# A two-layer transformer kernel: q and k roles in one copy, splits in three slots, masks and row additions moved on GpSimd, and a reordered opening

## The chip, the core and the metric

The kernel runs on one core of a Trainium2 chip. The metric is device time of one execution in microseconds (us). The time before is 1002.51 us, the median of 3 runs (996.39 to 1004.47). The engines are named as the profile names them: PE (matrix multiplies) and PEld (its weight loads), DVE (VectorE), ACT (ScalarE), POOL (GpSimd), and SP, whose queue SPq issues every DMA of this kernel.

## What is computed

Two transformer layers over 4 sequences of 512 tokens with 256 channels, 16 heads of 16 channels, and a feed-forward width of 1024. Layer 0 has a modulated norm, a dense additive bias of 4 x 16 x 512 x 512 numbers and a key mask; layer 1 is causal and is blended with its input by a gate per sequence.

```python
# layer 0
emb = silu(sin_emb(timestep)) @ W_ada + b_ada; scale, shift = split(emb)
x = ln(src) * (1 + scale) + shift
scores = q @ k.T / sqrt(16) + attention_bias;  scores = where(mask, -inf, scores)
x = x + softmax(scores) @ v @ Wo + bo
x = x + gelu2(ln(x) * g2 + beta2 ...) @ W2 + b2      # gelu2(a) = a * sigmoid(1.702 a)
# layer 1, for input x
h = ln(x) * gamma1 + beta1
x1 = x + softmax(where(causal, q @ k.T / 4, -inf)) @ v @ Wo + bo
x2 = x1 + gelu(ln(x1) * gamma2 + beta2 ...) @ W2 + b2
out = x + g * (x2 - x)
```

## The kernel before

Each engine has an instruction stream written out by hand, with semaphores between them. The work runs in phases: an opening; four X phases, each the attention of one sequence in layer 0; four Y phases, each the attention of one sequence in layer 1; and an end. The order is start, X -1, X 0, Y 0, X 1, Y 1, X 2, Y 2, Y 3, end. Phase X b does the attention of sequence b + 1 in layer 0, and Y b that of sequence b in layer 1. A phase is a loop over slots: 64 in X (one query tile of one head each), 96 in Y. The dense work of other sequences (norms, projections, output, feed-forward) is woven into the slots by the table `PLANS`: a field such as `qk=46, qk_by=2` is the slot at which PE starts the first q projection and the distance to the next. On each engine a `Stream` is a generator that yields the slot at which its next piece is due. Inside an engine everything is in order, so an instruction that waits holds all behind it.

Scores need more than bf16, so q and k are each cut into three bf16 parts (high, middle, low) and multiplied with six pairs of parts in one contraction over 96 rows (`Q_ROLE`, `K_ROLE`). ACT writes the high part (`keep_high`); DVE makes the others (`split`: the remainder L1290, which also frees PE's psD bank, the middle part L1293, the low part L1295). Then SP spreads the parts over partitions by copies inside the on-chip memory (`to_roles`, L409): for each half c of the heads six copies into q6 and then six into k6. Scores of heads 0 to 7 wait for the copies of c=0, those of heads 8 to 15 for c=1. One projection has four splits (q and k of two halves).

In an X phase SP loads a 128 x 512 bias tile for each slot into a ring of 12 (L374), POOL adds the mask to it (L554, six slots ahead: `MASK_AHEAD`), DVE adds the scores and takes the row maximum (L1340), ACT subtracts (L669), PE transposes (L937), ACT takes the exponential (L678), and PE multiplies with the values (L950). In a Y phase PE makes scores (L959), DVE finds row maxima (L1355), those are cut in parts, turned by PE, copied out by ACT (L708) and put by SP into three further rows of q6 against rows of ones in k6 (`max_rows`, L414); eight heads later PE makes the transposed scores (L969), ACT the exponential (L690), POOL zeroes the upper triangle (L593), and PE multiplies with the values (L981).

At the end of a Y phase POOL runs `set_x1` (L562, x1 = input + bo) and then, where another X phase with a new sequence follows (Y 0 and Y 1), the masks of that sequence's first six tiles:

```python
the_rest(dense, Y_SLOTS)
set_x1(b)
if b + 2 < B:
    for s in range(MASK_AHEAD):
        add_mask(b + 2, s)
```

In the opening PE starts with the embedding product (L1107), DVE adds its bias (L1205), PE spreads it over partitions (L869), ACT stores it (L728), DVE modulates (L1233, L1237), PE transposes (L863) and projects q, k (L877) and v (L884). POOL meanwhile reorders the weights (L543), fills the values with ones (L624), adds masks, adds bo (L562), fills k6's rows of ones (L630) and reorders layer 1's weights (L543).

## Time and profile before

| | |
|---|---|
| median of 3 runs | 1002.51 us (996.39 to 1004.47) |
| profiled execution | 1004.48 us, its span 1002.4 us |
| PE busy | 824.2 us (82%) |
| DVE busy | 611.7 us (61%) |
| ACT busy | 497.8 us (50%) |
| POOL busy | 417.0 us (42%) |
| HBM read | 86.28 MB, 88 GB/s over the span |

The span is what the trace covers; the rest of the time lies around it. Busy shares are averages over stages with different limits. Rows below come from the chain of waits (the work that ended last, followed back), from timelines (start in us, duration in us, engine, line, operation, out<-in, count, and in brackets the idle time before and what ended it), and from groups by line.

### The profile page before, as it was taken

How to read it: one execution, taken by the hardware profiler on the slowest of the kernel's cores; microseconds unless marked ns; L12 is line 12 of the kernel's file. 1: busy time of each engine (PE TensorE's matmuls, PEld its weight loads, DVE VectorE, ACT ScalarE, POOL GpSimd, SP SyncE). 2: the span in 40 equal slices, each digit the busy share in tenths (PEclk: the TensorE clock that was granted, in tenths of full speed). 3: DMA queues.
4: the chain of work that ended last, by engine and by line, in shares of the span. 5: the costliest groups of instructions: out<-in, count | busy, mean ns of one | idle time of the engine just before them, and what ended most of it. 6: DMA issues, size and time to landing. Idle time of an engine off the chain costs nothing.

```text
span 1002.4 us, 14648 instructions
## 1 busy us (share of the span) xinstructions
PE 824.2 (82%) x4830; PEld 492.6 (49%) x4830; DVE 611.7 (61%) x1693; ACT 497.8 (50%) x879; POOL 417.0 (42%) x422
## 2 busy tenths in 40 slices
PE   3577888789866877898998887888999897699768
PEld 1254456447532433566645533566556363446235
DVE  5899875675757824657847843666846654536121
ACT  1167786656712355666732445667742335044421
POOL 3946459655302129486402228486601113022320
PEclk9879999999995897999998997999999999889879
DMA  8476777434550024356551035455421115100000
GB/s 252 123 235 193 225 266 200 137 105 135 151 168 1 1 64 137 116 170 199 182 155 43 2 98 145 124 170 189 150 73 43 43 44 147 43 1 2 22 1 21
DMA packets 84154, 114.70 MB, mean 114 GB/s; under 512 B 9800, under 2 KB 49516, under 8 KB 84080
## 3 DMA queue, kind: packets, MB, share of 16 engines
q1 hardware_dynamic: 84080, 113.77, 37.6%
q8 instruction: 39, 0.64, 0.3%
q14 instruction: 35, 0.29, 0.1%
HBM read 86.28 MB, written 2.10 MB: 88 GB/s over the span
## 4 chain that ended last, share of the span: by engine, by line
PE 60%; DVE 21%; issue 8%; ACT 8%; POOL 2%; SPq 1%; DMA 0%; DVEq 0%; ACTq 0%; POOLq 0%
PE psD L905 11%; PE psD L917 11%; PE psE L937 6%; PE psC L981 5%; PE psC L950 4%; PE psD L877 4%; DVE tiles L1340 4%; PE psS L929 4%; PE psD L893 3%; PE psS L959 3%; PE psE L969 3%; PE psD L884 2%; ACT prob L678 2%; ACT prob L690 2%; DVE junk L1355 2%
## 5 line engine op out<-in xcount | busy, mean ns | idle before, releaser
L554 POOL TENSOR_TENSOR tiles<-tiles,mask_neg 128x512 f32<-128x512 f32 x240 | 281.9, 1204 | 89.0 <-DMA tiles<-in_fside_Bx16xSxS 71.0
L1340 DVE CUSTOM_DVE_ANT_0 tiles<-psS,tiles 128x512 f32<-128x512 f32 x256 | 174.1, 688 | 136.2 <-PE psS L929 102.1
L669 ACT ACTIVATE tiles<-tiles,rmax 128x512 f32<-128x512 f32 x224 | 161.6, 722 | 75.7 <-DVE rmax L1340 74.6
L678 ACT ACTIVATE prob<-psE 128x512 f32<-128x512 f32 x256 | 150.9, 595 | 96.8 <-PE psE L937 88.5
L1355 DVE CUSTOM_DVE_ANT_0 junk<-psS,later 128x128 bf16<-128x128 f32 (+3 forms) x256 | 121.0, 489 | 121.3 <-PE psS L959 120.5
L937 PE MATMUL psE<-ident,tiles 128*128 128x128 f32 x1024 | 161.5, 281 | 8.3 <-ACT prob L678 6.8
L937 PEld LDWEIGHTS psE<-ident,tiles 128*128 128x128 f32 x1024 | 129.1, 145 | 64.2 <-ACT prob L678 27.1
L690 ACT ACTIVATE prob<-psE 128x512 f32<-128x512 f32 (+1 forms) x192 | 95.5, 526 | 118.2 <-PE psE L969 117.3
L905 PE MATMUL psD<-hT,w 128*128 128x512 f32 x256 | 132.8, 630 | 17.5 <-DVE work L1281 13.6
L593 POOL TENSOR_SCALAR_AFFINE_SELECT prob<-prob 128x256 f32<-128x256 f32 x128 | 53.3, 440 | 220.8 <-ACT prob L690 220.8
L917 PE MATMUL psD<-w,work 128*128 128x256 f32 x512 | 134.0, 387 | 5.8 <-ACT hT L721 4.8
L929 PE MATMUL psS<-k,q 96*128 96x512 bf16 x256 | 101.4, 399 | 32.4 <-DVE rmax L1340 32.1
L959 PE MATMUL psS<-k,q 96*128 96x128 bf16 (+3 forms) x256 | 78.5, 323 | 32.9 <-DVE rmax L1355 27.3
L559 POOL TENSOR_TENSOR rstd<-var_eps,neg_half 128x4 f32<-128x4 f32 x16 | 16.6, 1036 | 207.6 <-DVE var_eps L1176 207.6
L917 PEld LDWEIGHTS psD<-w,work 128*128 128x128 f32 x512 | 91.9, 193 | 20.7 <-ACT hT L721 6.0
L969 PE MATMUL psE<-q,k 99*128 99x512 bf16 (+3 forms) x256 | 65.5, 312 | 19.1 <-ACT prob L690 18.3
L905 PEld LDWEIGHTS psD<-hT,w 128*128 128x128 f32 x256 | 45.1, 199 | 56.8 <-issue 34.1
L950 PE MATMUL psC<-prob,vx 128*32 128x256 f32 x1024 | 64.7, 395 | 1.0 <-ACT prob L678 1.0
L959 PEld LDWEIGHTS psS<-k,q 96*128 96x128 bf16 x256 | 25.2, 100 | 77.8 <-DVE rmax L1355 50.8
L929 PEld LDWEIGHTS psS<-k,q 96*128 96x128 bf16 x256 | 25.5, 100 | 65.6 <-DVE rmax L1340 46.0
L981 PE MATMUL psC<-prob,vx 128*32 128x128 f32 (+3 forms) x512 | 49.5, 539 | 1.5 <-POOL prob L593 1.4
L750 ACT ACTIVATE work<-psD,cols 128x512 f32<-128x512 f32 x32 | 22.0, 687 | 54.7 <-PE psD L905 54.7
(112 smaller groups left out, 953.6 us busy)
## 6 DMA issues: line engine op xcount, KB each, us to landing
tiles<-in_fside_Bx16xSxS SPq DMA_DIRECT2D x256, 256.0 KB, 2.7
q<-work SPq DMA_DIRECT2D x96, 128.0 KB, 2.7
k<-work SPq DMA_DIRECT2D x96, 128.0 KB, 2.4
w<-in_L_cond_W SPq DMA_DIRECT2D x12, 1024.0 KB, 5.5
res<-in_x SPq DMA_DIRECT2D x4, 512.0 KB, 5.6
out<-x SPq DMA_DIRECT2D x4, 512.0 KB, 5.0
mask_u<-in_mask_Bx1xSxS_bk SPq DMA_DIRECT2D x4, 256.0 KB, 3.1
q<-mT SPq DMA_DIRECT2D x48, 4.0 KB, 1.7
```

Source lines behind the costliest of these rows:

```text
L554: pool.tensor_tensor(tile(b, s), tile(b, s), mask_neg[:, tile_of(s)[1], :], ALU.add).then_inc(masked_p, 1)
L669: act.activation(tile(b, s), tile(b, s), ACT.Identity, scale=-1.0, bias=rmax[0][:, s:s + 1]).then_inc(shifted_a, 1)
L678: act.activation(prob0[:, part_no % 2, j, :, s % 2 * P:(s % 2 + 1) * P], psE[:, e_no(0, b, s) % 2, :].rearrange("p (k q) -> p k q", k=T), ...
L690: act.activation(prob1[:, h % KEEP, lo:hi], psE[:, n % 2, 0:hi - lo], ACT.Exp).then_inc(e_done, 1)
L905: mm = pe.matmul(psD[:, n % 2, :], w1[:, c, f * P:(f + 1) * P], hT2[:, c, :], start=c == 0, stop=c == C - 1)
L917: mm = pe.matmul(psD[:, n % 2, t % 2 * D:(t % 2 + 1) * D], gT[:, f, t * P:(t + 1) * P], w2[:, f, :], start=f == 0, stop=f == FC - 1)
L929: pe.matmul(psS[:, n % 2, :], q6[0:ROWS, h, t * P:(t + 1) * P], k6[0:ROWS, h, :], start=True, stop=True).then_inc(s_filled, 1)
L937: mm = pe.transpose(psE[:, n % 2, kt * P:(kt + 1) * P], tile(b, s)[:, kt * P:(kt + 1) * P], ident[:, :])
L950: mm = pe.matmul(psC[j * QW:(j + 1) * QW, half * S // 2:(half + 1) * S // 2], vx[0][:, kt, at:at + QW], prob0[:, part_no % 2, j, kt, :], s ...
L959: pe.matmul(psS[:, n % 2, 0:(t + 1) * P], q6[0:ROWS, h, t * P:(t + 1) * P], k6[0:ROWS, h, 0:(t + 1) * P], start=True, stop=True).then_inc( ...
L1340: dve.tensor_tensor_reduce(tile(b, s), psS[:, n % 2, :], tile(b, s), 1.0, -3e38, ALU.add, ALU.max, rmax[0][:, s:s + 1]).then_inc(s_drained, 1)
L1355: dve.tensor_tensor_reduce(junk[:, n % 2, 0:w], psS[:, n % 2, 0:w], later[:, S - w:S], 1.0, -3e38, ALU.add, ALU.max, rmax[1][:, h * T + t: ...
```

## The change

Seven things change. (1) q6 and k6 become one tensor qk6 with q and k side by side for each head, and `to_roles` copies q's part and k's part of a role in one DMA: 6 instead of 12 copies for each half. `max_rows` has 4 copies (one for each head) instead of 3. (2) `split` yields after each of its three DVE instructions, so they fall in three slots. (3) In Y phases `set_x1` and the six first masks of the next X phase get slots of their own (`x1=`, `masks=`). (4) The rows of ones are brought by a DMA from a constant table instead of POOL's memset L630. (5) On POOL `add_bo(0)` and layer 1's `swap_columns` move behind the opening, to slots 8, 12 and 16 of X -1, and the masks wait for the first norm. (6) DVE measures and turns the first mask before it modulates. (7) PE begins with 26 products of constants (`WARM_UP`), and in Y phases `store` stands before the last `max_rows`.

```diff
+WARM_UP = 26
-    ("Y", 0): Plan(tail=(0, 1), turn=5, out=(9, 10), ln2=13, t2=20,
+    ("Y", 0): Plan(x1=60, masks=44, tail=(0, 1), turn=5, out=(9, 10), ln2=13, t2=20,
...
-    ("Y", 1): Plan(tail=(0, 2), turn=5, out=(9, 12), ln2=15, t2=32,
+    ("Y", 1): Plan(x1=66, masks=44, tail=(0, 2), turn=5, out=(9, 12), ln2=15, t2=32,
...
-    ("Y", 2): Plan(tail=(0, 3), turn=5, out=(9, 12), ln2=15, t2=28,
+    ("Y", 2): Plan(x1=66, tail=(0, 3), turn=5, out=(9, 12), ln2=15, t2=28,
...
-    ("Y", 3): Plan(tail=(1, 2), turn=5, out=(9, 10), late=(1, 3, (3, 4)), ln2=13, t2=19,
+    ("Y", 3): Plan(x1=80, tail=(1, 2), turn=5, out=(9, 10), late=(1, 3, (3, 4)), ln2=13, t2=19,
...
-                for x, (dst, roles) in enumerate(((q6, Q_ROLE), (k6, K_ROLE))):
-                    for r, w in enumerate(roles):
-                        sp.dma_start(dst[r:ROWS:ROLES, c * H // C:(c + 1) * H // C, :], part[:, c, x, w, :]).then_inc(roles_in[c], 16)
+                for r, (i, j) in enumerate(zip(Q_ROLE, K_ROLE)):
+                    pair = part_row[:, c, i:PARTS + j + 1:PARTS + j - i, :]
+                    sp.dma_start(qk6[r:ROWS:ROLES, c * H // C:(c + 1) * H // C, :, :], pair).then_inc(roles_in[c], 16)
...
-                for w in range(PARTS):
-                    sp.dma_start(q6[ROWS + w:ROWS + w + 1, g * G:(g + 1) * G, :], mT[w * G * T:(w + 1) * G * T, g % 2, :]).then_inc(m_rows, 16)
+                for j in range(G):
+                    sp.dma_start(qk6[ROWS:SHIFT, g * G + j, 0, :], mT[j * PARTS * T:(j + 1) * PARTS * T, g % 2, :]).then_inc(m_rows, 16)
...
+                yield 28
+                sp.dma_start(qk6[ROWS:SHIFT, :, 1, :].bitcast(F32), ones_dram.rearrange("w (h n) -> w h n", h=H)).then_inc(ones_in, 16)
...
+                if at.ffn:
+                    store(at.ffn[1])
                 max_rows(b, 3)
...
-                if at.ffn:
-                    store(at.ffn[1])
...
+            def residual(b, at):
+                yield at.x1
+                set_x1(b)
+
+            def first_masks(b, at):
+                for s in range(MASK_AHEAD if b < B else 0):
+                    yield at.masks + 2 * s
+                    add_mask(b, s)
...
+            pool.wait_ge(norm_ready, T)
             for s in range(MASK_AHEAD):
                 add_mask(0, s)
-            add_bo(0)
-            pool.wait_ge(bo_added, 1)
-            pool.memset(k6[ROWS:SHIFT, :, :], 1.0).then_inc(ones_set, 1)
-            pool.wait_ge(ones_set, 3)
-            swap_columns(1)
+            def first_bo():
+                yield 8
+                add_bo(0)
...
-                    set_x1(b)
-                    if b + 2 < B:
-                        for s in range(MASK_AHEAD):
-                            add_mask(b + 2, s)
...
+            for _ in range(WARM_UP):
+                pe.matmul(psC[:, :], ident_b[:, :], later[:, :], start=True, stop=True)
             pe.wait_ge(ada_ready, 1)
...
+            mask_known = measure_mask(0)
             dve.wait_ge(ada_in, N_ADA)
             dve.wait_ge(ada_filled, 1)
...
+            turn_mask(0, mask_known)
             dve.wait_ge(small_ready, N_SMALL)
...
-            turn_mask(0, measure_mask(0))
```

POOL in the opening, before: two weight copies, the ones of the values, the inverse deviation, four masks, bo, the memset of k6, layer 1's weights, and then masks of X -1.

```order
L559 TENSOR_TENSOR rstd<-var_eps,neg_half 128x4
L554 TENSOR_TENSOR tiles<-tiles,mask_neg 128x512 x4
L562 TENSOR_TENSOR res<-res,bo_all 128x1024
L630 MEMSET k 3x8192
L543 TENSOR_SCALAR wq<-res 128x512
L543 TENSOR_SCALAR wk<-res 128x512
L554 TENSOR_TENSOR tiles<-tiles,mask_neg 128x512 x4
```

POOL at the same place after (L562 is now the mask addition, L570 the row addition, L551 the weights, L567 the inverse deviation).

```order
L567 TENSOR_TENSOR rstd<-var_eps,neg_half 128x4
L562 TENSOR_TENSOR tiles<-tiles,mask_neg 128x512 x8
L567 TENSOR_TENSOR rstd<-var_eps,neg_half 128x4
L562 TENSOR_TENSOR tiles<-tiles,mask_neg 128x512 x3
L570 TENSOR_TENSOR res<-res,bo_all 128x1024
L562 TENSOR_TENSOR tiles<-tiles,mask_neg 128x512 x3
L551 TENSOR_SCALAR wq<-res 128x512
L562 TENSOR_TENSOR tiles<-tiles,mask_neg 128x512 x2
L570 TENSOR_TENSOR res<-res,bo_all 128x1024
L562 TENSOR_TENSOR tiles<-tiles,mask_neg 128x512
L551 TENSOR_SCALAR wk<-res 128x512
```

The eight masks now stand together, the memset is gone, and bo and the weights stand between masks of X -1.

POOL at the end of Y 0, before: the last triangles (L593), then x1, then masks without a break into X 1.

```order
L593 AFFINE_SELECT prob<-prob 128x2x128
L593 AFFINE_SELECT prob<-prob 128x256
L562 TENSOR_TENSOR x<-res,bo_all 128x1024
L554 TENSOR_TENSOR tiles<-tiles,mask_neg 128x512 x24
L559 TENSOR_TENSOR rstd<-var_eps,neg_half 128x4
```

POOL in the second half of Y 0 after (L601 is now the triangle).

```order
L562 TENSOR_TENSOR tiles<-tiles,mask_neg 128x512 x2
L601 AFFINE_SELECT prob<-prob 128x2x128
L601 AFFINE_SELECT prob<-prob 128x256
L601 AFFINE_SELECT prob<-prob 128x2x128
L601 AFFINE_SELECT prob<-prob 128x256
L570 TENSOR_TENSOR x<-res,bo_all 128x1024
L601 AFFINE_SELECT prob<-prob 128x2x128
```

Six masks and x1 went from behind the last triangle to between triangles of earlier heads; the masks left behind it count 18.

DVE in Y 0 while sequence 2 is projected, before (L1355 is the row maximum of a score tile).

```order
L1355 ISA junk,rmax<-psS,later 128x384
L1355 ISA rmax 128x1
L1290 SCALAR_TENSOR_TENSOR work<-psD,cols,work 128x512
L1293 CAST work<-work 128x512
L1295 TENSOR_TENSOR work<-work 128x512
L1355 ISA junk,rmax<-psS,later 128x512
```

DVE at the same place after (L1380 is the maximum; L1332, L1336 and L1339 are the three steps of a split).

```order
L1332 SCALAR_TENSOR_TENSOR work<-psD,cols,work 128x512
L1380 ISA junk,rmax<-psS,later 128x384
L1380 ISA rmax 128x1
L1336 CAST work<-work 128x512
L1380 ISA junk,rmax<-psS,later 128x512
L1380 ISA rmax 128x1
L1339 TENSOR_TENSOR work<-work 128x512
```

Between the three steps of a split there is now a maximum each.

## Rows read from the trace of the kernel before

**Rows 1.** The page: the chain that ended last, shares of the span by engine

```profile
PE 60%; DVE 21%; issue 8%; ACT 8%; POOL 2%; SPq 1%; DMA 0%; DVEq 0%; ACTq 0%; POOLq 0%
```

**Rows 2.** Timeline of the opening: the embedding, modulation and first projections

```profile
11.04 3.58 PE L1107 MATMUL psM<-prob 128*4 128x512 f32 x4 [11.04 <-DVE prob L1201]
...
18.75 0.88 DVE L1233 SCALAR_TENSOR_TENSOR res<-res,mv,ada 128x256 f32<-128x256 f32 x2 [2.58 <-ACT ada L728]
...
22.17 2.28 DVE L1312 TENSOR_REDUCE mask_row<-mask_u 128x4 f32<-128x2048 uint8 x1
...
23.60 3.60 PE L877 MATMUL psD<-hT,wq 128*128 128x512 f32 x4 [0.56 <-ACT hT L721]
...
27.03 1.88 PE L877 MATMUL psD<-hT,wk 128*128 128x512 f32 x4
```

**Rows 3.** Timeline of the opening: POOL, DVE's splits, SP's copies, PE to the first score

```profile
34.35 6.92 POOL L630 MEMSET k<- 3x8192 bf16 x1
...
34.86 3.92 SPq L409 DMA_DIRECT2D q<-work  x6
35.53 6.02 DVE L1293 CAST work<-work 128x512 bf16<-128x512 f32 x1
...
41.35 1.97 POOL L543 TENSOR_SCALAR wq<-res 128x512 f32<-128x512 f32 x1
...
43.70 3.78 PE L884 MATMUL psD<-wv,hT 128*128 128x256 f32 x8 [6.09 <-DVE work L1290]
...
47.27 0.66 PE L929 MATMUL psS<-k,q 96*128 96x512 bf16 x2
```

**Rows 4.** Groups by line over the whole trace: min/median/max ns of one

```profile
L1293 DVE CAST work<-work x32: 426/428/6017, 28.8 to 842.6; 128x512 bf16<-128x512 f32 x32
...
L1295 DVE TENSOR_TENSOR work<-work x32: 691/693/2711, 29.3 to 843.0; 128x512 bf16<-128x512 f32 x32
...
L554 POOL TENSOR_TENSOR tiles<-tiles,mask_neg x240: 1143/1161/1640, 26.6 to 719.4; 128x512 f32<-128x512 f32 x120
```

**Rows 5.** DMA issues, and a large load's issue from the timeline of SP

```profile
q<-work SPq DMA_DIRECT2D x96, 128.0 KB, 2.7
...
tiles<-in_fside_Bx16xSxS SPq DMA_DIRECT2D x256, 256.0 KB, 2.7
...
829.11 0.58 SPq L396 DMA_DIRECT2D w<-in_L_cond_W  x1
```

**Rows 6.** Timeline at the boundary of X 0 and Y 0

```profile
275.55 3.79 SPq L409 DMA_DIRECT2D q<-work  x6
...
279.26 1.99 PE L884 MATMUL psD<-wv,hT 128*128 128x256 f32 x8 [0.32 <-DVE work L1290]
...
285.28 0.33 PE L959 MATMUL psS<-k,q 96*128 96x128 bf16 x2 [4.03 <-issue]
```

**Rows 7.** Timeline at the boundary of Y 0 and X 1

```profile
376.85 1.06 PE L929 MATMUL psS<-k,q 96*128 96x512 bf16 x2
...
378.34 2.34 POOL L562 TENSOR_TENSOR x<-res,bo_all 128x1024 f32<-128x1024 f32 x1
...
381.83 0.69 DVE L1340 CUSTOM_DVE_ANT_0 tiles<-psS,tiles 128x512 f32<-128x512 f32 x1 [6.27 <-POOL tiles L554]
...
385.08 4.14 PE L981 MATMUL psC<-prob,vx 128*32 128x512 f32 x32
```

**Rows 8.** Timelines: boundary of Y 1 and X 2; boundary of Y 2 and Y 3

```profile
610.65 0.69 DVE L1340 CUSTOM_DVE_ANT_0 tiles<-psS,tiles 128x512 f32<-128x512 f32 x1 [5.95 <-POOL tiles L554]
...
849.15 0.23 PE L959 MATMUL psS<-k,q 96*128 96x128 bf16 x1 [1.08 <-DMA k<-work]
```

**Rows 9.** Timeline of X -1: DVE's modulation beside POOL's masks, and POOL's idle time

```profile
63.34 2.34 DVE L1233 SCALAR_TENSOR_TENSOR res<-res,mv,ada 128x256 f32<-128x256 f32 x2 [0.25 <-ACT ada L728]
...
74.01 2.35 POOL L562 TENSOR_TENSOR res<-res,bo_all 128x1024 f32<-128x1024 f32 x1 [4.71 <-PE psD L863]
```

**Rows 10.** The chain that ended last, in order of time: a middle part of X 1

```profile
490.15 1.39 DVE work L1293
```

More of the change, by code:

```diff
@@ L73 @@
          (1, 1, 1), (1, 2, 0), (0, 3, 1), (1, 3, 0), (1, 2, 1), (1, 3, 1)]
-Plan = namedtuple("Plan", "tail turn out late ln2 t2 ffn f1 step f2 per early g1 g_step g2 g_per pre ln ada t1 qk qk_by v",
-                  defaults=(None,) * 23)
+Plan = namedtuple("Plan", "tail turn out late ln2 t2 ffn f1 step f2 per early g1 g_step g2 g_per x1 masks pre ln ada t1 qk qk_by v",
+                  defaults=(None,) * 25)
 PLANS = {
@@ L237, in two_layers @@
     freq_dram = freq_table.ap()
+    ones_table = nc.inline_tensor(np.full((PARTS, H * S // 2), 0x3F803F80, np.uint32).view(np.float32))
+    ones_dram = ones_table.ap()
     bias_dram = a["fside_Bx16xSxS_0"].rearrange("b h (t p) k -> (b h) t p k", p=P)
@@ L635, in _ @@
                 if kind == "X":
+                    if b < 0:
+                        dense += [Stream(first_bo()), Stream(swap_columns(1))]
                     for s in range(STEPS):
@@ L644, in _ @@
                 else:
+                    dense += [Stream(residual(b, PLANS[kind, b])), Stream(first_masks(b + 2, PLANS[kind, b]))]
                     for slot in range(Y_SLOTS):
@@ L1176, in spread, with measure_mask, turn_mask @@
                 dve.tensor_scalar(var_eps[:, :], mv[:, :, 1], EPS, None, ALU.add).then_inc(stats_ready, 1)
+            def measure_mask(b):
+                low, inf, nan = (mask_row[:, i, :] for i in range(3))
+                dve.wait_ge(mask_in, 16 * (b + 1))
+                last = mark(dve.tensor_reduce(low, mask_u8[:, :, :], AX_X, ALU.min))
+                dve.wait_ge(v_step, last)
+                last = mark(dve.tensor_scalar(inf, low, 3e38, 1e3, ALU.mult, ALU.mult))
+                dve.wait_ge(v_step, last)
+                return mark(dve.tensor_tensor(nan, inf, inf, ALU.subtract))
+            def turn_mask(b, last):
+                if b:
+                    dve.wait_ge(masked_p, masks(b - 1, STEPS - 1, False))
+                    dve.wait_ge(masked_v, masks(b - 1, STEPS - 1, True))
+                dve.wait_ge(v_step, last)
+                for t in range(T):
+                    ins = dve.tensor_scalar(mask_neg[:, t, :], mask_u8[:, t, :], -BIG, mask_row[:, 2, t:t + 1], ALU.mult, ALU.add)
+                ins.then_inc(mask_ready, 1)
             dve.wait_ge(step_in, 32)
@@ L1282, in gated, with split @@
                                          op0=ALU.add, op1=ALU.mult).then_inc(drained_v, 1)
-            def split(l, b, i):
+            def split(l, b, i, at):
                 c, x = divmod(i, 2)
@@ L1306, in keep_values @@
                                   ALU.add).then_inc(drained_v, 1)
-            def measure_mask(b):
-                low, inf, nan = (mask_row[:, i, :] for i in range(3))
-                dve.wait_ge(mask_in, 16 * (b + 1))
-                last = mark(dve.tensor_reduce(low, mask_u8[:, :, :], AX_X, ALU.min))
-                dve.wait_ge(v_step, last)
-                last = mark(dve.tensor_scalar(inf, low, 3e38, 1e3, ALU.mult, ALU.mult))
-                dve.wait_ge(v_step, last)
-                return mark(dve.tensor_tensor(nan, inf, inf, ALU.subtract))
-            def turn_mask(b, last):
-                if b:
-                    dve.wait_ge(masked_p, masks(b - 1, STEPS - 1, False))
-                    dve.wait_ge(masked_v, masks(b - 1, STEPS - 1, True))
-                dve.wait_ge(v_step, last)
-                for t in range(T):
-                    ins = dve.tensor_scalar(mask_neg[:, t, :], mask_u8[:, t, :], -BIG, mask_row[:, 2, t:t + 1], ALU.mult, ALU.add)
-                ins.then_inc(mask_ready, 1)
             def add_mask(b, s):
@@ L1358, in split_max @@
             def split_max(b, g):
-                m = rmax[1][:, g * G * T:(g + 1) * G * T]
-                high, middle, low = (mparts[:, g % 2, w, :] for w in range(PARTS))
-                left = rneg[:, g % 2, :]
+                m = rmax[1][:, g * G * T:(g + 1) * G * T].rearrange("p (h t) -> p h t", h=G)
+                high, middle, low = (mparts[:, g % 2, :, w, :] for w in range(PARTS))
+                left = rneg[:, g % 2, :, :]
                 dve.wait_ge(s_drained, s_no(1, b, G * T * (g + 1)))
@@ L1436, in projections @@
                 for i in range(2 * C):
-                    yield at.qk + i * at.qk_by + 2
-                    split(l, b, i)
+                    yield from split(l, b, i, at.qk + i * at.qk_by + 2)
                 for i in range(2 if at.v else 0):
@@ L1485, in _ @@
                 modulate(0, half)
-            turn_mask(0, measure_mask(0))
             for i in range(2 * C):
-                split(0, 0, i)
+                Stream(split(0, 0, i, 0)).upto(LAST)
             dve.wait_ge(ones_set, 2)
```

29 lines of the change are left out of this document (17 added, 12 removed).

## The prediction

> **What bounds the kernel now.** I read first the chain of waits by engine: PE has 60% of it, DVE 21%, POOL 2% [rows 1]. So most of the time is PE's own work, which the change leaves as it is, and what can be won lies where the chain leaves PE. I then read the timelines at the start and at each boundary between phases, looking in the brackets for idle times of several us. There are four kinds. In the opening the chain runs through DVE's splits, and the first score starts only at 47.27 [rows 3]. At X 0 to Y 0 PE stands still for 4.03 us [rows 6]. At Y 0 to X 1 and Y 1 to X 2 DVE waits 6.27 and 5.95 us for masks of POOL [rows 7, 8]. At Y 2 to Y 3 PE waits 1.08 us for the copies of k [rows 8]. The slots between boundaries repeat PE's pace, so a boundary that comes earlier moves all behind it by as much.
>
> **Opening.** Three things end before the first score: the last split frees a bank for the second v projection (PE starts it at 43.70 and is done near 47.3), the copies of c=0, and PE itself [rows 3]. One middle part of a split (L1293) takes 6.02 us at 35.53; the shortest of its kind takes 0.43 [rows 3, 4]. It ends just after POOL's memset of k6 (34.35 + 6.92 = 41.27) [rows 3]. The longest low part (L1295), the one before it, takes 2.71 us where others take 0.69 [rows 4]; it lies beside POOL's addition of bo. The change takes the memset and that addition away from here. In their place POOL puts eight masks of 1.16 us in a row [rows 4], which start when the norm is done, at about 22.3 (18.75 + 4 x 0.88 [rows 2]), and last to about 32. So I take 0.6 for the middle part (between 0.43 alone and 0.43 + 1.16 behind one mask) and 1.5 for the low part (0.69 + 0.8 of a mask): 5.4 + 1.2 = 6.6 us less before the second v projection, which then starts at 37.1. It took 3.78 us after an idle time of 6.09 and takes 1.99 without one [rows 3, 6], so it is done between 39.1 and 40.9.
>
> The copies: before, twelve for each half, the six q copies issued in 3.92 us [rows 3] and the six of k in as much, so 7.8 us. A copy now carries 256 KB instead of 128. An issue does not follow the size: one of 128 KB takes 0.65 us (3.92 / 6), a weight load of 1024 KB in pieces takes 0.58 [rows 3, 5]. Nor does the landing: 2.7 us after the issue for both 128 and 256 KB [rows 5]. So I take 0.65 for each, 3.9 us for six. They started at 34.86 [rows 3]; now 1.2 us earlier, 33.6 + 3.9 + 2.7 = 40.2. Both paths meet at about 40.2: 7.1 us less. The Trainium skill, DMA: Bandwidth & Descriptors (section Anatomy of one DMA), gives a fixed part of 2.0 us and bytes over 436 GB/s for a DMA issued by GpSimd; as an estimate by that page the landing would grow by 0.3 us and the sum shrink by as much at each boundary. The upper bound of the copy is twice the issue, 1.3 us each: then 44.1 and a gain of 3.2.
>
> The 26 products of constants fill PE from about 3 us on. Without them the first projection, four products, takes 3.60 us and the next four 1.88 [rows 2]: PE runs the first at its lower clock level (1.2 GHz) and the second at the higher (2.4 GHz). What the products can win on the path is 1.7 us there and 1.7 at the embedding product (3.58 for four). But PE is idle again between embedding, transposes and projection, and the gain at the embedding is lost to DVE: the mask's reduction of 2.28 us [rows 2] now stands before the addition that waits for that product. The product is released at 11.04, so this addition can't start before 13.3, and with the norm's statistics between it starts about where it did, 14.62 (11.04 + 3.58 [rows 2]). The turns of the mask, which stood behind the reduction, fall into DVE's wait of 2.58 us before it modulates at 18.75 [rows 2]. A bf16 product of 512 columns takes 0.33 us (0.66 / 2 [rows 3]), 26 of them 8.6; if the first 3.6 us are slow, as those of the projection are, six of them take 3.6 and the rest 6.6, and they end near 13, 2.0 us late. Bounds -2.0 to +1.7; I take +0.5, since half of the first projection may run fast. Opening: 7.6 us.
>
> **X -1.** What left the opening comes back here: bo (2.35 us by its twin [rows 9]) and the two weight copies, 1.97 us each [rows 3], 6.3 us of POOL. POOL has room: it waits 4.71 us before 74.01 [rows 9], and masks are six slots ahead. But DVE is slowed beside it: two modulating instructions take 2.34 us beside masks [rows 9] and 0.88 in the opening [rows 2]. Four such pairs, two of which were beside POOL before, may lose 1.46 each: 0 to 4 us. I take 2.5. That DVE waits for a whole POOL instruction is what the memset's row shows [rows 3, 4]. The Trainium skill, SBUF — State Buffer (section Who interferes with whom), has it as an exclusive lock: casts, and DVE instructions with two SBUF inputs against a reading GpSimd instruction, wait for the other to end. By that rule a move of POOL work wins nothing by itself, only its place counts; it speaks against the moves into X -1, and the whole moved 6.3 us could come back in X -1.
>
> **X 0 to Y 0.** PE ends v at 281.25 (279.26 + 1.99) and starts Y 0 at 285.28 [rows 6]. Between lies the landing of k's last copy: copies start at 275.55, where the split is just done, and 7.7 + about 2.1 later the score starts. With six copies the last lands at 275.55 + 3.9 + 2.7 = 282.1. Gain 3.2, bounds -0.8 (issue doubled: 275.55 + 7.8 + 2.7) and 4.0 (PE is next). The same at Y 2 to Y 3: PE's wait of 1.08 us goes [rows 8]; 1.1. At the other boundaries the copies of c=0 are early and nothing is won.
>
> **Y 0 to X 1, Y 1 to X 2.** DVE could use the first scores at about 377.3 (376.85 + one product), and starts at 381.83, behind POOL's 2.34 us for x1 and the first mask [rows 7]. With both done in the Y phase that is 4.5 us, and the same at 610.65 against about 606.1 [rows 8]: 4.5. From 385.08 the product with the values takes 4.14 us [rows 7]; whether PE keeps its higher clock there with less idle time I leave out, bounds 0 to +1.8 each. Sum 9.0. What carries them now: a slot of Y 0 lasts 0.95 us (91.57 us from 285.28 to 376.85 for 96 slots [rows 6, 7]); six masks of 1.16 with two slots each fit, and x1 takes 2.5 slots where a triangle is due each fourth. x1 waits for the store of the sequence before, queued behind SP's third `max_rows` (its maxima are out at slot 52); behind the waiting POOL stand triangles, and PE waits for those. From slot 52 to x1 at slot 66 it is 13 us, against 2.7 for the landing of 256 KB [rows 5] and twice the size here. Cost taken 0.5 for all Y phases (0 to 2).
>
> **Splits in three slots.** Beside a mask a middle part takes 1.39 us, and such pieces are on the chain [rows 10]; now a maximum stands between two parts. The parts are not shorter, and the remainder that frees the bank comes at the same slot. If two middle parts of four go from the chain in each of the three later X phases, 6 x 1.39 = 8.3 us go. I take 2.5 with bounds 0 to 8, since PE's own work holds the next slot in most places (60% of the chain [rows 1]). The low parts come two slots later, but the copies of c=0 are asked for at that very slot. The fourth `max_rows` copy, the row copies of ones and the order of `store` cost nothing: their readers come twelve slots later.
>
> **Sum.** 7.6 - 2.5 + 3.2 + 1.1 + 9.0 - 0.5 + 2.5 = 20.4 us. The profiled execution took 1004.48, 2.1 above its span of 1002.4, and 2 above the median. The sum is a difference, so it goes off both: 984.1 for a profiled run like this one, and 1002.5 - 20.4 = 982.1 off the median. I forecast 982.
>
> **Rivals.** (A) The copies cost by bytes: 1.3 us an issue. Then the opening gains 3.2 (first score at 44.1), X 0 to Y 0 loses 0.8, Y 2 to Y 3 gains nothing: 3.2 - 2.5 - 0.8 + 9.0 - 0.5 + 2.5 = 10.9, so 992. For it: the pair of pieces has one dimension more. Against: the 1024 KB load. (B) POOL's work comes back in X -1 in full, by waits of DVE for whole instructions, and the splits win nothing: 20.4 - 3.8 - 2.5 = 14.1, so 988. For it: DVE is the busiest there. Against: POOL's 4.71 us of idle. (C) PE's clock: the warm-up holds (+1.2), both value products run fast (+3.6), splits win 6 (+3.5): 28.7, so 974. For it: clock drops follow idle times, which shrink. (D) Slower: a paired copy holds SP much longer, 2.4 us, six 14.4 us. Then the first score is at 33.6 + 14.4 + 2.7 = 50.7, 3.4 later than before; Y 0's at 275.55 + 17.1, 7.4 later; Y 3's 6.6 later (14.4 - 7.8), and the other four boundaries, whose copies are asked for somewhat ahead, I price at 2 each: 25.4 lost against 8.5 that stays of the rest (9.0 - 0.5 + 2.5 - 2.5), so 1019. It decides from an issue of about 1.9 us on, where the lost and the won are equal. No row shows one: the dearest has 0.65. (E) The change does not do what it says, each boundary being held by something that ends just behind (ACT's exponentials; POOL's last triangle, which ends where x1 begins, 378.34 [rows 7]): half of the 9.0 and the 3.2 comes, 14.3, so 988.
>
> **How the numbers follow.** Forecast as worked out (976 to 987) 0.52, C 0.15, A 0.10, B and E 0.17, D 0.03, a rest of small effects with no visible change 0.03. The range takes in C below and A, B and E above, with the bounds of opening and X -1: 970 to 993. A difference of 1%, about 10 us, is what a measurement of this kernel can tell. Faster by over 1% (below 992.5): the forecast, C, nearly all of B and E, half of A, 0.84; within 1% 0.13; slower by over 1% 0.03.
>
> **What would show it.** In the profile after: the first score near 40 instead of 47.3, no middle part above 1.7 us in the opening; SP's six copies of a half in about 4 us; Y 0's first score about 1 us after v; DVE's first maximum of X 1 and X 2 within 1 us of the first score and no POOL row of x1 at the end of Y; X -1 longer by 2 to 3 us from its first score to that of X 0. I would be wrong if an issue takes over 1 us, if X -1 grows by the whole of what the opening lost, or if POOL waits in Y for the store.

## The result and the profile after

The changed kernel takes 997.51 us (median of 20 runs, 988.06 to 1001.61), the kernel before 1002.1 beside it (20 runs, 996.39 to 1011.3). The ratio is 0.9959, 95% interval 0.9942 to 0.9977: some 4 us less, where 20.4 were forecast, and outside the range given (970 to 993). The profiled execution took 1000.84, its span is 999.0. Medians here are over all runs of a kernel, while the ratios leave out single runs over 1.5% above the kernel's fastest, of which four of the kernels below have one each.

The opening answers to [rows 2, 3]. Timeline of the kernel after (start, duration, engine, line, operation, count, in brackets the idle time before and what ended it):

```profile
7.69 2.54 PE L1124 MATMUL psC<-later,ident_b 128*128 128x512 bf16 x11
...
12.56 3.11 PE L1128 MATMUL psM<-prob 128*4 128x512 f32 x4 [2.34 <-DVE prob L1240]
...
24.66 3.75 PE L894 MATMUL psD<-hT,wq 128*128 128x512 f32 x4 [0.56 <-ACT hT L738]
...
32.83 0.60 DVE L1336 CAST work<-work 128x512 bf16<-128x512 f32 x1
...
33.46 1.53 DVE L1339 TENSOR_TENSOR work<-work 128x512 bf16<-128x512 f32 x1
...
35.02 9.11 SPq L414 DMA_DIRECT2D qk<-work  x12
...
35.80 3.75 PE L901 MATMUL psD<-wv,hT 128*128 128x256 f32 x16 [0.96 <-DVE work L1332]
...
44.91 1.03 PE L946 MATMUL psS<-qk 96*128 96x512 bf16 x2 [5.36 <-DMA qk<-work]
```

PE has both v projections done at 39.55 (35.80 + 3.75), where before it was there near 47.3: the middle part that took 6.02 us beside POOL's memset takes 0.60. Then PE waits 5.36 us for the copies, and the last bracket says so. The last of the six lands at 44.86, 9.84 us after the first issue, and the first score comes at 44.91, where 40.2 was forecast.

How long the copies take is in section 6 of the page (operation, count, KB each, median us from issue to landing), to be read against [rows 5]:

```profile
tiles<-in_fside_Bx16xSxS SPq DMA_DIRECT2D x256, 256.0 KB, 2.9
qk<-work SPq DMA_DIRECT2D x96, 256.0 KB, 5.8
```

A tile of 256 KB lands 2.9 us after its issue, a pair of 256 KB 5.8. The DMA view of one half's copies before (362.4 to 372.1 us), then of the same half after (365.8 to 375.5): packets, MB, share of the engines' time, and the landing.

```profile
q1 hardware_dynamic: 1792, 1.58, 59.3%
...
q<-work SPq DMA_DIRECT2D x6, 128.0 KB, 2.4
k<-work SPq DMA_DIRECT2D x6, 128.0 KB, 2.4
```

```profile
q1 hardware_dynamic: 1519, 1.58, 81.0%
...
qk<-work SPq DMA_DIRECT2D x6, 256.0 KB, 4.9
```

Both windows are 9.7 us long and move 1.58 MB. The issues of six pairs take 4 us, but the landings then come 1.2 to 1.3 us apart.

The boundaries answer to [rows 6 to 8]. First X 0 to Y 0, then Y 0 to X 1, in the timeline after:

```profile
270.79 4.86 SPq L414 DMA_DIRECT2D qk<-work  x6
...
274.13 1.99 PE L901 MATMUL psD<-wv,hT 128*128 128x256 f32 x8 [0.32 <-DVE work L1332]
...
276.47 4.76 SPq L414 DMA_DIRECT2D qk<-work  x6
...
282.49 0.48 PE L976 MATMUL psS<-qk 96*128 96x128 bf16 x2 [6.36 <-issue]
```

```profile
380.00 1.06 PE L946 MATMUL psS<-qk 96*128 96x512 bf16 x2
...
380.78 0.69 DVE L1365 CUSTOM_DVE_ANT_0 tiles<-psS,tiles 128x512 f32<-128x512 f32 x1 [2.09 <-PE psS L946]
...
382.54 1.06 PE L954 MATMUL psE<-ident,tiles 128*128 128x128 f32 x4
```

At X 0 to Y 0 PE waits 6.36 us after v, where it waited 4.03; the last pair of that half lands at 282.40, 0.1 us before the score. At Y 0 to X 1 DVE takes the first maximum 0.78 us after the first score starts, where it was 4.98 (381.83 less 376.85 [rows 7]): the 4.5 us forecast are there. At Y 1 to X 2 it is 0.89 us.

Y 0 itself is longer. The windows view gives a stretch, its length, each engine's busy time with its count (PE, PEld, DVE, ACT, POOL), PE's granted clock, the DMA share and GB/s. Y 0 and the stretch from the middle of Y 3 to the end, before and then after:

```profile
285.30:376.90 91.60, 68.16 (x351) 32.00 (x352) 57.29 (x205) 31.65 (x66) 19.32 (x34) 0.80 0.14 39
896.90:1002.40 105.50, 83.69 (x436) 50.06 (x434) 30.80 (x109) 37.21 (x70) 20.80 (x36) 0.91 0.03 11
```

```profile
282.50:380.00 97.50, 72.43 (x351) 34.59 (x352) 57.41 (x205) 31.77 (x66) 28.46 (x41) 0.76 0.16 32
890.50:999.00 108.50, 87.21 (x436) 51.94 (x434) 30.80 (x109) 37.26 (x70) 20.74 (x36) 0.87 0.03 11
```

PE runs the same 351 and 436 instructions and is busy 4.3 and 3.5 us longer, at a granted clock of 0.76 instead of 0.80 and 0.87 instead of 0.91. In one profile this looks like a cost of the change of 9 us. Whether it is one, the experiments had to say.

### The profile page after: what moved, and what is told of

It reads as the page before. It is cut to its first block, busy times and chain, and to the rows that moved or that the text cites. A ratio compares the mean times of both kernels' runs of the same rounds, so it can differ in the third digit from the quotient of the medians.

```text
span 999.0 us, 14619 instructions
## 1 busy us (share of the span) xinstructions
PE 835.1 (84%) x4856; PEld 497.1 (50%) x4856; DVE 603.3 (60%) x1693; ACT 496.6 (50%) x879; POOL 409.4 (41%) x421
## 4 chain that ended last, share of the span: by engine, by line
PE 62%; DVE 19%; issue 8%; ACT 7%; DMA 2%; SPq 1%; POOL 1%; DVEq 0%; ACTq 0%
PE psD L922 11%; PE psD L934 11%; PE psE L954 7%; PE psC L998 5%; PE psC L967 4%; PE psS L946 4%; PE psD L894 4%; PE psD L910 3%; PE psS L976 3%; DVE tiles L1365 3%; PE psE L986 3%; PE psD L901 2%; ACT prob L707 2%; DVE junk L1380 2%; ACT prob L695 1%
## 5 line engine op out<-in xcount | busy, mean ns | idle before, releaser
L562 POOL TENSOR_TENSOR tiles<-tiles,mask_neg 128x512 f32<-128x512 f32 x240 | 282.7, 1204 | 89.6 <-DMA tiles<-in_fside_Bx16xSxS 73.1
L1380 DVE CUSTOM_DVE_ANT_0 junk<-psS,later 128x128 bf16<-128x128 f32 (+3 forms) x256 | 121.4, 488 | 126.2 <-PE psS L976 125.7
L922 PE MATMUL psD<-hT,w 128*128 128x512 f32 x256 | 130.4, 620 | 18.3 <-DVE work L1322 14.6
L601 POOL TENSOR_SCALAR_AFFINE_SELECT prob<-prob 128x256 f32<-128x256 f32 x128 | 52.3, 433 | 201.7 <-ACT prob L707 201.7
L946 PE MATMUL psS<-qk 96*128 96x512 bf16 x256 | 102.3, 403 | 23.1 <-DVE rmax L1365 17.5
L567 POOL TENSOR_TENSOR rstd<-var_eps,neg_half 128x4 f32<-128x4 f32 x16 | 16.6, 1034 | 233.4 <-DVE var_eps L1196 233.4
L976 PE MATMUL psS<-qk 96*128 96x128 bf16 (+3 forms) x256 | 77.4, 321 | 39.2 <-DVE rmax L1380 31.1
L986 PE MATMUL psE<-qk 99*128 99x512 bf16 (+3 forms) x256 | 66.2, 315 | 18.4 <-ACT prob L707 17.6
L922 PEld LDWEIGHTS psD<-hT,w 128*128 128x128 f32 x256 | 44.4, 196 | 56.5 <-issue 33.2
L976 PEld LDWEIGHTS psS<-qk 96*128 96x128 bf16 x256 | 25.2, 100 | 83.0 <-DVE rmax L1380 52.7
L998 PE MATMUL psC<-prob,vx 128*32 128x128 f32 (+3 forms) x512 | 52.5, 565 | 1.4 <-POOL prob L601 1.4
L946 PEld LDWEIGHTS psS<-qk 96*128 96x128 bf16 x256 | 25.3, 100 | 55.4 <-DVE rmax L1365 29.3
L986 PEld LDWEIGHTS psE<-qk 99*128 99x128 bf16 x256 | 23.7, 100 | 50.5 <-ACT prob L707 30.6
```

Source lines behind the costliest of these rows:

```text
L562: pool.tensor_tensor(tile(b, s), tile(b, s), mask_neg[:, tile_of(s)[1], :], ALU.add).then_inc(masked_p, 1)
L922: mm = pe.matmul(psD[:, n % 2, :], w1[:, c, f * P:(f + 1) * P], hT2[:, c, :], start=c == 0, stop=c == C - 1)
L946: pe.matmul(psS[:, n % 2, :], q6[0:ROWS, h, t * P:(t + 1) * P], k6[0:ROWS, h, :], start=True, stop=True).then_inc(s_filled, 1)
L976: pe.matmul(psS[:, n % 2, 0:(t + 1) * P], q6[0:ROWS, h, t * P:(t + 1) * P], k6[0:ROWS, h, 0:(t + 1) * P], start=True, stop=True).then_inc( ...
L986: mm = pe.matmul(psE[:, n % 2, lo:lo + w], k6[0:SHIFT, h, kt * P:(kt + 1) * P], q6[0:SHIFT, h, kt * P:S], start=True, stop=True)
L1380: dve.tensor_tensor_reduce(junk[:, n % 2, 0:w], psS[:, n % 2, 0:w], later[:, S - w:S], 1.0, -3e38, ALU.add, ALU.max, rmax[1][:, h * T + t: ...
```

## Experiments

Ratios are to the kernel before on the same chip, with the 95% interval. "Single copies" is the changed kernel with twelve copies of 128 KB for a half instead of six of 256.

**Single copies.**

```diff
-for r, (i, j) in enumerate(zip(Q_ROLE, K_ROLE)):
-    pair = part_row[:, c, i:PARTS + j + 1:PARTS + j - i, :]
-    sp.dma_start(qk6[r:ROWS:ROLES, c * H // C:(c + 1) * H // C, :, :], pair)
+for x, (dst, roles) in enumerate(((q6, Q_ROLE), (k6, K_ROLE))):
+    for r, w in enumerate(roles):
+        sp.dma_start(dst[r:ROWS:ROLES, c * H // C:(c + 1) * H // C, :], part[:, c, x, w, :])
```

> The changed kernel with twelve copies for each half again instead of six pairs; the joint tensor and all else stay. Theory T (the copies are bound by the transfer itself, since 1.5 MB of a half took 9.4 to 10 us from first issue to last landing both in six and in twelve copies): each copy lands about 2.5 us after its issue again, the last of a half again 9.5 to 10 us after the first issue, the first score and the boundary of X 0 and Y 0 stay within 1 us of the changed kernel, and the time within 0.3% of it (ratio to before 0.993 to 0.999). Rival R (the pairs are a loss, since a landing of 5.8 us keeps both q and k late and blocks SP's queue for the tile loads behind): 3 to 6 us faster than the changed kernel, ratio 0.989 to 0.993.

Measured 991.18 us, ratio 0.9885 (0.9848 to 0.9922). Its page and its timeline:

```profile
qk<-work SPq DMA_DIRECT2D x192, 128.0 KB, 2.5
```

```profile
44.49 1.04 PE L946 MATMUL psS<-qk 96*128 96x512 bf16 x2 [5.15 <-DMA qk<-work]
...
281.08 0.48 PE L976 MATMUL psS<-qk 96*128 96x128 bf16 x2 [4.32 <-issue]
```

The first score is where the pairs had it, as the theory of an unchanged landing said, but the whole is 6 us faster, as its rival said. PE's wait at X 0 to Y 0 is 4.32 us and not 6.36. So pairs win nothing and cost something elsewhere.

**The Y part alone**: kernel before, with x1 and the first masks in the Y phases and the earlier store.

> The kernel before with one part of the change: x1 and the six first masks in slots of the Y phases, and the store before the last copy of maxima. Theory T (this part carries the gain): the wait of DVE for masks at the start of X 1 and X 2 goes, 4.5 us each, and the time is 7 to 9 us below before, ratio 0.991 to 0.993; the rest of the change then loses what it wins. Rival R (PE's clock takes it back: POOL's work and less idle time move the clock in the Y phases): ratio 0.996 to 1.000, with Y 0 longer by some us than 91.6.

993.47 us, 0.9915 (0.9884 to 0.9945): 8.5 us, as forecast for it (9.0 less 0.5). Its Y 0 is 96.7 us long instead of 91.6, as the rival said.

**The splits in three slots alone.**

> The kernel before with the three steps of a split in three slots. Theory T (PE's own work holds the next slot nearly everywhere): within 2.5 us of before, ratio 0.997 to 1.000. Rival R (lumps of 2 to 3.4 us on DVE were on the chain): 5 to 8 us less, ratio 0.992 to 0.995. A second rival: the parts ready two slots later hold SP and the copies, ratio above 1.001.

996.05 us, 0.9927 (0.9902 to 0.9951): 7.3 us, where 2.5 were taken.

**The opening alone**, with the joint tensor, the row copies, and single copies.

> The kernel before with the opening of the change alone (products of constants, mask first, ones by transfer, bo and layer 1's weights in X -1) and the joint tensor with twelve copies and four copies of maxima. Theory T (the copies of c=0 hold the first score, since they can't land before 9.5 us after the first part): first score 44 to 45.5, 2 to 3 us less than before, X -1 the same or up to 3 us shorter since POOL's backlog of masks is gone, ratio 0.995 to 0.998. Rival R (moved POOL work comes back in X -1): X -1 longer by 2 us and more, ratio 0.998 to 1.002.

999.1 us, 0.9979 (0.995 to 1.0009): 2 us of the forecast 7.6 less 2.5, and the interval takes in no change at all.

**Y part and splits together.**

> The kernel before with two parts of the change alone: the x1 and mask work inside the Y phases, and the splits in three slots. Theory T (the two act at different places, X boundaries and stretches of splits, and add): 9.5 + 7 us less, about 986, ratio 0.984. Rival N (single ratios of half a per cent are partly chance of the clock, or both win at the same wait of DVE for POOL): about 991, ratio 0.989, no better than the changed kernel with single copies.

991.91 us, 0.9898 (0.9851 to 0.9946). The rival's number: 10 us, where the two alone add up to 16.

**Single copies, no products of constants.**

```diff
-WARM_UP = 26
+WARM_UP = 0
```

> The changed kernel with single copies, without the 26 products of constants. Theory T (in the changed kernel they end at 10.2 us, PE is idle again before the first projection, which takes 3.75 us for four products as before): first score within 0.5 us of 44.5, ratio as with them, 0.9885. Rival C (they hold PE's clock for what follows): the embedding product longer by 0.5 us or more, first score over 45.5, ratio above 0.990.

991.05 us, 0.9893 (0.9859 to 0.9926), first score 45.0. No gain of the products can be told from the time (0.9885 and 0.9881 with them). Something they do: without them the embedding product takes 3.57 us; with them it takes 1.88, PE's pace at the higher level, in five of ten profiles, those in which PE stood idle for 1.1 to 1.5 us before it, and 2.3 to 3.1 in the five with 2.0 to 2.6 us of idle. The first projection takes 3.4 to 3.75 us in all ten.

**Rows together**: the pairs, each written to 16 neighbouring partitions; the scores sum the same terms in another order.

```diff
-sp.dma_start(qk6[r:ROWS:ROLES, c * H // C:(c + 1) * H // C, :, :], pair)
+sp.dma_start(qk6[r * DH:(r + 1) * DH, c * H // C:(c + 1) * H // C, :, :], pair)
```

> The changed kernel, with the pairs, but each copy writes 16 neighbouring partitions instead of 16 that lie six apart. Theory T (the six copies are bound by the total of the packets, 3072 of 1 KB for a half, at whatever partitions): last landing of a half 9.4 us after the first issue, as before, time within 0.3% of 997.5. Rival L (the layout of the destination sets the packet's 86 ns): the landing changes by 2 us or more in one direction, and the first score, 44.9, with it.

1039.79 us, 1.0375 (1.0331 to 1.0419). The page, and the first score in the timeline:

```profile
qk<-work SPq DMA_DIRECT2D x96, 256.0 KB, 11.6
```

```profile
51.13 1.03 PE L946 MATMUL psS<-qk 96*128 96x512 bf16 x2 [12.04 <-DMA qk<-work]
```

The DMA view of one half (380.4 to 396.6 us), to be read against the 1.58 MB in 9.7 us above:

```profile
q1 hardware_dynamic: 1600, 1.66, 93.4%
```

The theory of a limit by bytes or packets alone falls (a half has 1536 packets of 1 KB, not the 3072 of its text). The layout sets the rate: the six of the first half take 4.7, 6.3, 8.1, 9.8, 11.4 and 13.1 us from issue to landing, and as they are also issued 0.7 us apart, the landings come 2.36 us apart instead of 1.28. The last one comes 16.5 us after the first issue instead of 9.8.

**Pairs alone**: kernel before with the joint tensor, pairs and row copies.

> The kernel before with the joint tensor, its paired copies and the row copies that the joint tensor needs, nothing else of the change. Theory T (a half takes as long in six copies as in twelve, but all its bytes are asked for at once, so tile loads of that stretch land late and PE's clock falls): first score of X -1 within 0.5 us of 47.3, landings of tiles over 5 us in more than 30 places instead of 15, ratio 1.003 to 1.008. Rival S (the loss in the changed kernel comes from the pairs together with its other moves, or is chance): ratio 0.998 to 1.002, as many late tiles as before.

1001.67 us, 1.0006 (0.9974 to 1.0039); behind the opening, 31 tiles land over 5 us after their issue instead of 15 (43 and 34 in the two profiles of the changed kernel, 22 and 22 with single copies). Late tiles are there, a loss is not to be seen: by the time the rival is right, by the tiles the theory. The forecast had the pairs at 4.3 us won at two boundaries and 3 to 4 in the opening.

**The changed kernel again, and single copies again**, on one chip.

> The changed kernel once more, unedited, on the chip of the next run. Theory P (the pairs cost 6 us inside the changed kernel): ratio 0.996 again, and the single copies on the same chip 0.6 to 0.8% below it. Rival V (two stretches whose time hangs on where PE's clock falls, Y 0 with 90 to 100 us and the end with 105.5 or 108.5, differ from build to build and run to run, and the pairs cost nothing): the two come within 0.4% of each other.

> The changed kernel with single copies once more. Theory P: ratio 0.9885 plus or minus 0.003, below the changed kernel's in this call by 0.6 to 0.8%. Rival V: 0.992 to 0.995, within 0.4% of it.

996.76 us, 0.9918 (0.9885 to 0.9951), and 993.22, 0.9881 (0.9834 to 0.9929). The gap is 0.37%, just inside what the rival allowed. Over all runs the changed kernel has a mean of 996.54 (31 runs) and single copies, with this run's twin of the first test, 992.47 (12 runs): 4.1 us apart, plus or minus 2.9 (twice the standard error; 4.9 by the runs that the ratios use). With the kernels without constants and with two issuers, also of single copies, it is 3.9 plus or minus 2.2 (30 runs; 5.0 by the runs that the ratios use). The pairs cost something in the whole, less than the first pair of medians said. The profile of the rerun has the same two stretches as above:

```profile
283.50:380.20 96.70, 71.11 (x351) 32.57 (x352) 58.19 (x205) 31.79 (x66) 28.41 (x41) 0.76 0.16 32
890.30:995.70 105.40, 83.58 (x436) 49.97 (x434) 30.81 (x109) 37.11 (x70) 20.69 (x36) 0.91 0.03 11
```

The end takes 105.4 us here and took 108.5 in the first profile of the very same kernel. So the 3.0 us more there (108.5 after 105.5) are no effect of the change.

**Two issuers**: single copies; in the opening SP issues those of q and ACT those of k.

```diff
+for c in range(C):
+    act.wait_ge(parts_ready, 2 * c + 2)
+    for r, w in enumerate(K_ROLE):
+        act.dma_start(k6[r:ROWS:ROLES, c * H // C:(c + 1) * H // C, :], part[:, c, 1, w, :]).then_inc(roles_in[c], 16)
```

> The changed kernel with single copies; in the opening alone SP issues the twelve of q and ACT the twelve of k, which it did nothing beside. Theory T (transfers are the limit, 256 KB in 1.2 us whoever asks for them): landings grow within the half to some 5 us, the last one comes 9 to 9.7 us after the first issue, first score 44.5. Rival I (twelve single copies are held by their issue of 0.6 us, and a pair's packets are slow for their form): the last landing comes 6 to 7 us after the first issue, first score near 42, 2 to 3 us less in all.

992.33 us, 0.9878 (0.9834 to 0.9922). Timeline, and the DMA view from 35.4 to 45.2 us:

```profile
35.52 8.87 SPq L414 DMA_DIRECT2D qk<-work  x12
35.52 8.60 ACTq L847 DMA_DIRECT2D qk<-work  x12
...
45.29 1.04 PE L950 MATMUL psS<-qk 96*128 96x512 bf16 x2 [5.23 <-DMA qk<-work]
```

```profile
qk<-work SPq DMA_DIRECT2D x12, 128.0 KB, 6.3
qk<-work ACTq DMA_DIRECT2D x12, 128.0 KB, 6.1
```

Issued twice as fast, single copies land as late as pairs: the last of the half 9.7 us after the first issue. In this layout 256 KB take 1.2 to 1.3 us, whoever asks for them.

**A plain delay** of the kernel before, by four memsets on DVE at its start.

> The kernel before with four memsets on DVE ahead of its first step, a plain delay of the opening by some 2 to 4 us that can be read at the first score; nothing else differs. Theory V (stretches hang on where PE's clock falls in time): Y 0 or the end changes its length by 2 us or more against 91.6 and 105.5 with no edit there, and the time moves by another amount than the delay. Rival D (only the edits at a stretch set its length): every stretch within 1 us of before, time above before by the delay, ratio 1.002 to 1.004.

1008.93 us, 1.0065 (1.0031 to 1.0099). The timeline, and the two stretches in the windows view:

```profile
5.61 0.91 DVE L1180 MEMSET work<- 128x1024 f32 x1 [5.61 <-DMA freq<-freq_table]
...
53.11 1.06 PE L929 MATMUL psS<-k,q 96*128 96x512 bf16 x2
```

```profile
288.60:385.10 96.50, 71.68 (x351) 34.20 (x352) 57.26 (x205) 31.75 (x66) 19.18 (x34) 0.77 0.14 38
901.50:1007.00 105.50, 83.68 (x436) 50.09 (x434) 30.80 (x109) 37.16 (x70) 20.74 (x36) 0.91 0.03 11
```

The first score comes 5.84 us later (53.11 less 47.27), and the median is 5.2 us above that of the runs beside it (1008.93 less 1003.69); by the ratio it is 6.5. Yet Y 0, which nothing was done to, is 96.5 us long instead of 91.6, at a clock of 0.77, and Y 1 gives 3.5 back (98.4 instead of 101.8). Both theories are half right: over many runs the delay arrives whole, and in one profile a stretch is off by 5 us for no edit. The 5.84 us are more than the four memsets of 0.91: the start of the opening scatters too, see below.

**Opening and splits; opening and Y part** (both with single copies).

> The kernel before with the new opening (single copies) and the splits in three slots; x1 and the masks stay where they were. Alone these two gave 0.9979 and 0.9927. Theory A (the parts add, and what misses in the whole is the scatter of single ratios): 0.991, 9.5 us less. Theory O (they overlap: the POOL work that the opening hands to X -1 takes back what the splits win there, X -1 is 100 to 102 us and not 98.7): 0.9935 to 0.997.

> The changed kernel with single copies and the splits in one slot as before: new opening and the x1 and mask work in the Y phases. Alone these gave 0.9979 and 0.9915. Theory A: 0.9895, and the splits are worth next to nothing on top of it (the whole has 0.9885). Theory O (only opening and splits collide): 0.9895 too, and X -1 102 to 103. A rival of both, K (the splits stay worth 7 us in the whole): 0.995.

995.9 us, 0.9929 (0.9891 to 0.9967), and 995.77, 0.9905 (0.9873 to 0.9938). The first lies between its two theories, with an X -1 of 101.6 us as theory O said; the second has an X -1 of 102.7. From the second to the whole (0.9885, 0.9881) the splits are worth 2 us, not 7.

**POOL's work in the opening again**: single copies, with bo and the two weight copies taken out of X -1.

```diff
-def first_bo():
-    yield 8
-    add_bo(0)
+add_bo(0)
+Stream(swap_columns(1)).upto(LAST)
...
-if b < 0:
-    dense += [Stream(first_bo()), Stream(swap_columns(1))]
```

> The changed kernel with single copies, but bo and the two weight copies of POOL come in the opening again, behind its masks, where it has nothing to do from 34.2 us on, and X -1 is free of them. Theory O: first score within 0.7 us of 44.5, since the copies hold it and not the splits, X -1 98 to 99.5 instead of 100.6 to 101.7, ratio 0.986, 2 to 3 us below the kernel with single copies. Rival H (they slow the last splits, c=1 and v come late, and X -1 has room for them): first score 46 or more, X -1 unchanged, ratio 0.988 to 0.991.

989.5 us, 0.9864 (0.982 to 0.9907), the lowest median of all, though the interval takes in 0.9885 too. Its timeline, and X -1 in the windows view:

```profile
26.61 2.34 POOL L570 TENSOR_TENSOR res<-res,bo_all 128x1024 f32<-128x1024 f32 x1
...
32.89 5.32 POOL L562 TENSOR_TENSOR tiles<-tiles,mask_neg 128x512 f32<-128x512 f32 x4
...
42.75 1.04 PE L943 MATMUL psS<-qk 96*128 96x512 bf16 x2 [4.14 <-DMA qk<-work]
```

```profile
42.80:141.50 98.70, 81.47 (x587) 50.55 (x588) 85.36 (x194) 73.98 (x130) 53.16 (x43) 0.92 0.76 237
```

The same stretch with the work in X -1 (single copies):

```profile
44.50:146.20 101.70, 83.69 (x586) 51.29 (x587) 88.78 (x194) 73.66 (x130) 60.03 (x46) 0.90 0.73 231
```

The copies still hold the first score, so the work costs nothing in the opening, and DVE is busy 3.4 us less in X -1. This kernel also has 32 late tiles.

## Why the prediction was wrong, step by step

**The step that failed** is "Nor does the landing: 2.7 us after the issue for both 128 and 256 KB", with the sum built on it, "3.9 us for six" + 2.7. The row for 256 KB [rows 5] is that of a tile, which comes from HBM and goes to 128 partitions; a role copy goes to 16. The six issues did take 4 us. But the landings come 1.2 to 1.3 us apart, and in the opening the last one comes 9.84 us after the first issue, where 6.6 were forecast and twelve single copies had taken 9.66. (Over the sixteen halves it is 9.5 to 9.9 us in seven and up to 14 in the others.) The single copies landed a steady 2.4 us after their issue, one every 0.65 us, and 128 KB take 0.6 at the rate of the pairs: the two limits lay side by side, and halving the issues uncovered the other. A DMA share of 59% in that window before looks like room, and was none: it became 81% at the same 163 GB/s. The two issuers settle it.

Of the 4.7 us by which the first score missed 40.2, 3.2 are this landing and 1.4 the start of the copies (35.02 where 33.6 was forecast). The start is for the most part scatter: in eleven profiles with the new opening it lies at 33.1 to 35.5, mean 34.5, in five with the old one at 34.9 to 36.5, mean 35.6, so the 1.2 us forecast there came, and [rows 3] was an early case. One source of it can be seen: DVE's steps ahead of the embedding product wait 0.76 us for a small load in the profile after, and not in the one before. The same holds for the 2.4 us between the two first scores (47.27 to 44.91): the means are 47.9 (five profiles) and 44.4 (nine, with pairs or single copies, POOL's work not in the opening), so 3.5 of the forecast 7.1 came. With v done early the copies now hold the score alone. X 0 to Y 0 lost 2.3 us in PE's wait instead of winning 3.2, and at Y 2 to Y 3 the wait for the copies stands at 1.28 us in the timeline instead of 1.08. Rival A had the first score nearly right (44.1) for the wrong reason: the bytes cost, not at the issue but at the landing. Its total of 992 is still 5.5 us too low.

By the Trainium skill, DMA: Bandwidth & Descriptors (section Anatomy of one DMA), the landing should have grown by 0.3 us; the medians are 2.5 and 5.8. The page that bears on it is another. The Trainium skill, SBUF — State Buffer (section Door 1: The DMA port swizzle) says that a transfer's rate goes by how many of 16 ports its partitions reach, gives the map, and 27.2 GB/s for a port. By that map 16 neighbouring rows reach 4 ports: as an estimate by that page 256 KB take 2.4 us, and 2.36 was measured. Here the trace agrees. 16 rows six apart reach 13 or 14 ports, for which the same estimate gives 0.7 us, and 1.2 to 1.3 was measured: the number of ports does not give this rate. The fullest of them holds two of the 16 rows, and an eighth of 256 KB through one port gives an estimate of 1.2 us. That the fullest port sets the pace fits both layouts; no other layout was run to test it.

**Pairs in the whole** cost 4 us more than single copies. Two of these can be placed: at X 0 to Y 0 the half that the score waits for lands 11.6 and 11.8 us after its first issue in the two profiles of the changed kernel and PE waits 6.4 and 6.6 us, against 9.5 to 10.4 and 4.0 to 4.9 in five kernels with single copies. With pairs SP starts the next half's copies while the first is still landing (276.47 against a last landing at 282.40). Why this costs time there is open: pairs alone did the same and had 9.9 and 4.6. Late tiles alone do not make a kernel slow: the two fastest by ratio (POOL's work in the opening, two issuers) have 32 and 34 of them.

**X -1, -2.5.** X -1 took 102.6 us before (101.3 to 102.8 in four profiles with neither part). With splits in slots and without POOL's added work it takes 98.7 to 99.4 (three kernels), with both 99.9 to 101.9 (seven profiles, mean 100.9), with the added work alone 102.7 and 102.9. The added 6.3 us cost 2, near the 2.5 taken, and the last experiment, by one profile, says that it need not be paid. Of rival B's full return a third came. By the Trainium skill, SBUF — State Buffer (section Who interferes with whom), a DVE cast in one of its faster modes and a POOL instruction exclude each other, and the later one waits for the whole of the other; the longest middle part, a cast, fell from 6.0 to 1.4 us once the memset was gone, which agrees.

**Splits, +2.5.** Right mechanism, size too small: 3 to 4 us in X -1, a stretch for which I had counted nothing, and 7.3 for the kernel by themselves; 5 on top of the opening, 2 on top of the Y part, 2 on top of both. The bounds given, 0 to 8, hold all of these.

**Y to X, 9.0 less 0.5.** The mechanism is right: the first turn of X 1 comes 2.5 us after the first score instead of 7.2. The 8.5 us by itself agree in part by luck. In ten profiles with this part (rows together left out) X 1 and X 2 are 6.3 and 4.3 us shorter than in six without it (means 120.7 and 121.7 after 126.9 and 126.0), more than the 9.0 forecast, and Y 0 is 3.9 us longer, where 0.5 was taken for all Y phases. On top of the splits the part is worth 3 us, on top of opening and splits 4 to 5.

**Clock and constants.** The 26 products ended at 10.2 us and not near 13, the projection still took 3.75 us at the lower of the two levels, and without them the time is the same within its interval. I had taken them at 0.5 us won, with -2.0 to +1.7 as bounds. Y 0 has 95.6 to 99.9 us in nine of ten profiles with the Y part (92.6 in the tenth; rows together left out) and 90.2 to 94.3 in five of six without it (96.5 in the delayed kernel). With the same product counts most of this is PE's clock (4.3 of 5.9 us in the windows above), and it takes back some 4 us of what the Y part wins at its boundaries. The delayed kernel shows that it can come without any edit; what decides it is open.

**The sum.** Opening 0.9979, Y part 0.9915 and splits 0.9927 multiply to 0.982; the whole with single copies has 0.988, 6 us less gained. Two of the 6 are X -1's. Splits and Y part together miss their own sum by as much (10.2 us for 15.8), but the intervals of the parts, some 3 to 5 us each, leave room for chance: a plain fit of eight ratios (the three parts, their pairings, and the whole with single copies twice) by three terms gives 1.4 us for the opening, 6.8 for the Y part and 5.5 for the splits, 2 us either way, and no ratio lies more than 1.5 standard errors off. So the single ratios of Y part and splits were probably too good, and a loss where the parts meet is shown for X -1 alone. Y 0's clock is no reason for it: the Y part by itself already has a Y 0 of 96.7 us. Taken from the single ratios, the forecast of 20.4 comes apart like this: the opening gave 3.0 less (2.1 for 7.6 - 2.5), the copies' boundaries 4.3 less and the pairs took 4 besides, the splits alone gave 4.8 more, and 6 are missing from the sum of the parts: 20.4 - 3.0 - 4.3 - 4 + 4.8 - 6 = 7.9, against 4.1 and 8.2 by the two ratios of the changed kernel. Each term is uncertain by some 3 us.

## What to carry to other kernels

A landing time holds for the layout it was read from. Whether issue or transfer sets the pace of a row of copies is told neither by the issue times nor by a DMA share below 1, but by asking for them from two engines at once. Take the price of a stretch from several profiles before laying 3 us of it to an edit, and where an engine waits for a transfer anyway, put other engines' spare work there rather than into the next phase.

## What the hardware showed beyond that

Copies inside the on-chip memory to 16 partitions six apart moved 256 KB in 1.2 to 1.3 us (205 to 213 GB/s), issued by one queue or two, while a tile load of the same size from HBM landed in 2.9 us. To 16 neighbouring partitions they took 2.36 us (111 GB/s), and the kernel 3.75% longer. One kernel's last 105 us took 105.4 or 108.5 us, with PE busy 83.58 or 87.21 us over the same 436 instructions.
